# Scattering one coded value per edge and counting over 80 half-target buckets in a graph-transformer kernel

## What is computed

```python
# layer 0, graph part: x is the normalised input, (625, 1024)
out = x @ root + bias
for r in range(8):
    mask = (edge_type == r)
    sums = segment_sum(x[src] * mask, dst, 625)
    cnt = segment_sum(mask, dst, 625)
    out = out + (sums / max(cnt, 1)) @ weight[r]
z = concat([out, x]) @ w_gate + b_gate
h = tanh(out) * z + x * (1 - z)
# beside it: linear attention on x (qkv, 16 heads), then a quantised MLP; layer 1 is of the same kind
```

## Time and profile before

| | us |
|---|---|
| median of 3 runs | 1878.79 |
| lowest, highest | 1878.29, 1881.19 |
| span of the profiled execution | 1878.8 |
| TensorE busy in it | 1794.9 |
| VectorE busy in it | 1023.3 |
| ScalarE busy in it | 478.5 |
| GpSimd busy in it | 701.1 |

### The profile page before, as it was taken

How to read it: one execution, slowest core, us unless ns; L and a number is a source line. 1 busy time by engine, 2 the same in 40 slices (tenths; PEclk the granted TensorE clock), 3 DMA queues, 4 the chain that set the end, 5 groups by cost and what they waited for, 6 DMA issues and landing times.

```text
span 1878.8 us, 28666 instructions
## 1 busy us (share of the span) xinstructions
PE 1794.9 (96%) x9953; PEld 1477.4 (79%) x9953; DVE 1023.3 (54%) x2540; ACT 478.5 (25%) x1055; POOL 701.1 (37%) x609
## 2 busy tenths in 40 slices
PE   6999999999999999999999999954999999999999
PEld 4876689987777778787777887742899888878987
DVE  7888999997254543526354356786632224362311
ACT  3139956662010110101011145243100000111100
POOL 2110000003634435353534444200485552345862
PEclk9999999999999999999999999956999999999999
DMA  4532222224213121231313534110354351113322
GB/s 134 154 109 77 73 86 79 75 67 129 91 38 89 45 72 56 66 86 47 94 33 113 172 84 131 45 46 7 96 164 146 104 156 51 37 55 118 90 73 66
DMA packets 129282, 162.23 MB, mean 86 GB/s; under 512 B 14288, under 2 KB 75368, under 8 KB 128922
## 3 DMA queue, kind: packets, MB, share of 16 engines
q1 hardware_dynamic: 100848, 120.93, 21.5%
q10 hardware_dynamic: 22250, 23.53, 4.0%
q0 software_dynamic: 6080, 16.40, 2.9%
HBM read 135.51 MB, written 25.30 MB: 86 GB/s over the span
## 4 chain that ended last, share of the span: by engine, by line
PE 84%; DVE 6%; ACT 6%; issue 1%; DVEq 1%; DMA 1%; POOL 0%; ACTq 0%; SPq 0%
PE ps L367 22%; PE ps L368 22%; PE ps L369 21%; PE ps L1236 9%; PE ps L892 3%; ACT sc_col L838 2%; ACT sc_row L837 1%; PE ps L1201 1%; DVE w_lo L318 1%; PE ps L881 1%; PE ps L1156 1%; DMA nat<-in_x 1%; ACT w_hi L313 1%; PE ps L1183 1%; PE ps L1211 0%
## 5 line engine op out<-in xcount | busy, mean ns | idle before, releaser
L367 PE MATMUL ps<-w_hi,xt_hi 128*125 128x512 f32 x1320 | 539.0, 408 | 9.1 <-DVE xt_lo L549 3.5
L256 POOL TENSOR_TENSOR w_hi<-w_stage,zero 128x512 fp32r<-128x512 f32 x256 | 276.8, 1081 | 684.4 <-PE ps L369 670.0
L368 PE MATMUL ps<-w_lo,xt_hi 128*125 128x512 f32 x1320 | 523.0, 396 | 0.0
L369 PE MATMUL ps<-w_hi,xt_lo 128*125 128x512 f32 x1320 | 521.5, 395 | 0.0
L259 POOL TENSOR_TENSOR w_lo<-w_stage,w_hi 128x512 fp32r<-128x512 f32 x256 | 346.2, 1352 | 20.1
L367 PEld LDWEIGHTS ps<-w_hi,xt_hi 128*125 128x125 f32 x1320 | 246.6, 187 | 67.1 <-DVE xt_lo L549 4.3
L369 PEld LDWEIGHTS ps<-w_hi,xt_lo 128*125 128x125 f32 x1320 | 246.0, 186 | 63.3
L368 PEld LDWEIGHTS ps<-w_lo,xt_hi 128*125 128x125 f32 x1320 | 246.3, 187 | 53.5
L367 PE MATMUL ps<-xt_hi,w_hi 128*128 128x314 f32 x736 | 250.5, 340 | 1.3 <-DVE ring L2430 0.6
L369 PE MATMUL ps<-xt_hi,w_lo 128*128 128x314 f32 x736 | 225.9, 307 | 0.0
L368 PE MATMUL ps<-xt_lo,w_hi 128*128 128x314 f32 x736 | 225.7, 307 | 0.0
(11 more groups left out here) (392 smaller groups left out, 2390.2 us busy)
## 6 DMA issues: line engine op xcount, KB each, us to landing
w_stage<-in_stream SPq DMA_DIRECT2D x374, 256.0 KB, 2.7
pre<-ring POOLq DMA_DIRECT2D x30, 250.0 KB, 3.8
a_qt<-pre_t SPq DMA_DIRECT2D x18, 312.5 KB, 3.8
a_qt<-pre_t ACTq DMA_DIRECT2D x14, 312.5 KB
pre_t<-ring_t POOLq DMA_DIRECT2D x12, 312.5 KB, 2.8
pre_t<-ring_t ACTq DMA_DIRECT2D x12, 312.5 KB
a_vx<-pre SPq DMA_DIRECT2D x9, 312.5 KB
nat<-pre SPq DMA_DIRECT2D x2, 1250.0 KB
```

Source lines behind the costliest of these rows:

```text
L256: POOL.tensor_tensor(w_hi[:, q, :], w_stage[:, q % NST, :], zero[:].to_broadcast([128, 512]), ALU.add).then_inc(S("hi_done"), 1)
L367: PE.matmul(dst, l_hi, r_hi, start=first, stop=False)
L368: PE.matmul(dst, l_hi, r_lo, start=False, stop=False)
L369: return PE.matmul(dst, l_lo, r_hi, start=False, stop=last)
```

## The change

- Buckets are halved by target: 80 of them, number 2 x (old bucket) + (target is 314 or more). Each is padded to chunks of 128, which again makes 240 chunks, in 120 pairs.
- Positions: the mask has 28 rows in place of 40. Three bucket numbers share a row, with weights 1, 256 and 65536, so that one running sum counts three. A second sum over 80 operations of 166 int16 values (`key_start`) gives each edge the start of its bucket.
- Scatter: target and source are packed in the upper 16 bits of a float32 (`e_code`), so that its bf16 value holds both. VectorE makes the masked table `sc_code` in one operation. ScalarE has no part in it. One matmul of 240 columns in place of two. `slot_keys` unpacks the bits.
- Count: `hot_col` is 314 wide and `hot_row` is made for four chunks at once (512 elements); one matmul of 314 columns for each chunk; one ScalarE copy for each pair; one add of 314 for each chunk, at a start that is read from `g_start` into registers, four at a time (`hist_starts`).
- `adj` is zeroed by VectorE just ahead of the scatter, no longer by ScalarE.
- Groups 0 to 3 are evacuated by ScalarE without a bias (`evacuate_plain`). Their biases are loaded late by SP (`load_bias_h`; the second pair behind a wait for `gsum`) and added by VectorE to `nat` and `z` (`bias_half`).
- GpSimd takes the splitting over at chunk 84 in place of 86.

```diff
     def scatter_dve(c, j):
         DVE.wait_ge(S("sc_pe"), c + 1)
-        if row_on_dve(j):
-            DVE.tensor_scalar(sc_row[j][:], iota16[0:P, 0:128], e_lo[:, bass.ds(c, 1)], e_row1[:, bass.ds(c, 1)],
-                              ALU.is_equal, ALU.mult)
         DVE.tensor_scalar(sc_hi[j][:], iota16[0:P, 0:NCHUNK], e_hi[:, bass.ds(c, 1)], None, ALU.is_equal)
-        DVE.tensor_scalar(sc_lo[j][:], iota16[0:P, 0:128], e_lo[:, bass.ds(c, 1)], None,
-                          ALU.is_equal).then_inc(S("sc_hot"), 1)
+        DVE.tensor_scalar(sc_code[j][:], iota16[0:P, 0:128], e_lo[:, bass.ds(c, 1)],
+                          e_code[:, bass.ds(c, 1)].bitcast(F32), ALU.is_equal, ALU.mult).then_inc(S("sc_hot"), 1)
...
+    def hist_hot(c):
+        if c % 4 == 0:
+            if c >= 8:
+                DVE.wait_ge(S("hi_pe"), c - 4)
+            DVE.tensor_tensor(hot_row[c // 4 % 2][:], iota_by4[:],
+                              slot_row[:, c:c + 4].unsqueeze(1).to_broadcast([128, 128, 4]), ALU.is_equal)
+        if c >= 8:
+            DVE.wait_ge(S("hi_pe"), c - 7)
+        DVE.tensor_scalar(hot_col[c % 8][:], col_key[:], slot_col[:, bass.ds(c, 1)], None,
+                          ALU.is_equal).then_inc(S("hi_dve"), 1)
...
+    def hist_add(c, start):
+        DVE.wait_ge(S("hi_main"), c // 2 + 1)
+        if c:
+            DVE.wait_ge(S("hi_add"), c)
+        o = adj[:, bass.ds(start, SPLIT)]
+        DVE.tensor_tensor(o, o, counts[c // 2 % 4][:, c % 2, :], ALU.add).then_inc(S("hi_add"), 1)
...
+                for c in (2 * (h * per + n), 2 * (h * per + n) + 1):
+                    hist_add(c, starts[c])
+                    if c + LEAD_HOT < NCHUNK:
+                        hist_hot(c + LEAD_HOT)
+                    if c % STARTS == 0 and c + STARTS < NCHUNK:
+                        starts.update(zip(range(c + STARTS, c + 2 * STARTS), hist_starts(c + STARTS)))
+                    if c % 2 == 0 and chunk_at(h, n):
+                        split_dve(chunk_at(h, n))
...
+        for b in range(NKEY):
+            DVE.tensor_scalar(key_start[:, b, :], e_key16[:], float(b), b_off[:, b:b + 1], ALU.is_equal, ALU.mult)
...
+        if c == C_GATE - 3:
+            SP.wait_ge(S("gsum"), 1)
+            load_bias_h(2)
...
     DVE.reciprocal(rgam[:], gam[:])
     DVE.drain().then_inc(S("rgam"), 1)
+    DVE.wait_ge(S("ld_z"), 32)
+    DVE.wait_ge(S("ld_bh"), 64)
+    for g in range(2):
+        bias_half(z, g)
```

More of the change, by code:

```diff
@@ L731, in bucket_counts @@
-        DVE.tensor_tensor_scan(scan[:].rearrange("p b c -> p (b c)"), kh, kh, 0.0, ALU.add, ALU.max)
+        DVE.scalar_tensor_tensor(e_key[:], e_key[:], 2.0, e_half[:], ALU.mult, ALU.add)
+        DVE.drain()
+        k_, row, first = e_key[:], e_row[:, 0:EC], e_first[:, 0:EC]
+        wide, narrow = e_wide[:, 0:EC], e_narrow[:, 0:EC]
+        DVE.tensor_copy(e_key16[:, 0:EC], k_)
+        DVE.tensor_scalar(first, k_, float(NROW), None, ALU.is_ge)
+        DVE.tensor_scalar(e_half[:], k_, float(2 * NROW), None, ALU.is_ge)
@@ L732, in bucket_counts @@
+        DVE.tensor_scalar(e_pos[:], e_col[:], float(SPLIT // 2), float(KEY1 - KEY0 - SPLIT // 2), ALU.is_ge, ALU.mult)
         DVE.drain()
-        DVE.memset(b_beg[:, 0:1], 0.0)
-        DVE.tensor_copy(b_beg[:, 1:NBUCKET], scan[:, 0:NBUCKET - 1, EC - 1])
+        DVE.tensor_tensor(e_col[:], e_col[:], e_pos[:], ALU.add)
+        DVE.scalar_tensor_tensor(row, first, -float(NROW), k_, ALU.mult, ALU.add)
+        DVE.tensor_scalar(wide, first, 2.0 ** 8 - 1.0, 1.0, ALU.mult, ALU.add)
+        DVE.tensor_scalar(narrow, first, 2.0 ** -8 - 1.0, 1.0, ALU.mult, ALU.add)
@@ L735, in bucket_counts @@
         DVE.drain()
-        DVE.tensor_tensor(b_tot[:], scan[:, :, EC - 1], b_beg[:], ALU.subtract)
+        DVE.scalar_tensor_tensor(row, e_half[:], -float(NROW), row, ALU.mult, ALU.add)
+        DVE.scalar_tensor_tensor(wide, e_half[:], 2.0 ** 16 - 2.0 ** 8, wide, ALU.mult, ALU.add)
+        DVE.scalar_tensor_tensor(narrow, e_half[:], 2.0 ** -16 - 2.0 ** -8, narrow, ALU.mult, ALU.add)
+        DVE.drain()
+        DVE.scalar_tensor_tensor(e_low[:], e_col[:], 128.0, e_low[:], ALU.mult, ALU.add)
@@ L910, in beside @@
         for g in range(3):
-            load_bias(g)
-            for c in range((g + 1) * KT, (g + 2) * KT):
+            ahead = (g + 2) * KT - (2 if g == 0 else 1)
+            for c in range((g + 1) * KT, ahead):
                 split_act(c)
-        load_bias(3)
+            evacuate_plain(g)
+            for c in range(ahead, (g + 2) * KT):
+                split_act(c)
         for c in range(C_HAND, C_HAND + 4):
             split_act(c)
-        wait(ALE, mk)
-        mk_zero = sig(ALE.activation(adj[:].bitcast(F32), zero[0:P, :].to_broadcast([P, NBUCKET * NB // 2]), ACT.Copy), "act_step")
+        evacuate_plain(3)
         dense(3)
@@ L952, in beside @@
         DVE.wait_ge(S("split_done"), NST + C_HAND)
[L953 to L956 removed]
+        assert SC0 == G_PLAIN
         for i in range(SC_GROUPS):
@@ L973, in beside, with idle @@
             if i == SC_GROUPS - 1:
[L974 removed]
                 DVE.wait_ge(S("sc_pe"), sc_per + EC + 1)
[L976 to L979 removed]
+                slot_keys()
+                for c in range(LEAD_HOT):
+                    hist_hot(c)
             evacuate(i + SC0)
[L982 to L983 removed]
         HI0 = SC0 + SC_GROUPS
         assert HI0 + HI_GROUPS == G_PRE0
[L986 to L987 removed]
+        per = NPAIR // HI_GROUPS
+        assert per * HI_GROUPS == NPAIR and per * 4 == KT * T * 3
+        def idle(h, s_):
+            return s_ in (1, 2) or s_ > 2 and s_ % 4 == 3 and 3 < s_ < 36 if h == 0 else s_ % (4 if h < HI_GROUPS - 1 else 8) == (
+                3 if h < HI_GROUPS - 1 else 7)
         def hist_of(h, s_):
[L990 to L992 removed]
+            n = sum(not idle(h, i) for i in range(s_))
+            return n if not idle(h, s_) and n < per else None
         def first_step(h, k):
```

392 lines of the change are left out of this document (214 added, 178 removed).

## The result

The changed kernel takes **1865.39 us** (median of four, 1864.44 to 1866.98), the kernel before beside it 1878.68: ratio 0.9925, interval 0.9913 to 0.9937. The forecast was 1866. The median agrees, but three of its terms were off, and their errors cancelled; most of what follows is on them.

A forecast was written before the change was run, and what follows sets the result against it. TensorE, busy in 96% of the span, was taken to bound the kernel, with VectorE pacing the count step. Terms +5.2 - 13.7 + 1 + 0.6 - 7.7 + 2 = -12.6 took 1878.8 to 1866 us; range 1846 to 1902.

The forecast's parts named there:

- Ahead of the scatter: VectorE's work before the scatter: 72.0 us added, 51.1 removed, 8.4 of waits closed; ready at 147.0, +5 us.
- Scatter: In the scatter, VectorE sets the pace at 5.22 us a weight chunk instead of 6.13: -13.7 us.
- clock and transition: Around the scatter: +1 us for TensorE's longer wait and clock, +0.6 for unpacking keys and masks before the count.
- the term of 1 us: At the scatter's start, TensorE's longer wait, about 7 us, costs 1 us more through the granted clock; bounds 0 and 3.
- Count step: In the count step, VectorE's masks, adds, own waits, register loads and splits need 179 us against 186.5: -7.7 us.
- 10.1 us of ends and gaps: In the count step, the part of 186.5 us left to the step's ends and small gaps, kept for the changed kernel.
- Rival (a): Count step: the load costs by the register, 60 loads add 20 to 40 us, giving 1886 to 1906; chance 0.30.
- neighbouring words: Count step: the argument against a load costing by the register, that the four words loaded are neighbours; no size.
- Rival (b): Count step: the wait for the own add is hidden, 0.1 not 0.22; 24 us less, 1842; chance 0.12.
- floor of 155 us: Count step: TensorE's least time, 186.5 us less 31 us for the halved count matmuls.
- Late biases: Late part: adds on z fit VectorE's idle 8.13 us, adds on nat cost nothing, loads delay weight chunks: +2 us.

The follow-up runs named there:

- the two experiments: The changed kernel without the late biases at all, 1856.2 us, and the changed kernel without only the two adds on z, 1861.5 us.

## Why the prediction was right, and where it wasn't

**Ahead of the scatter: the sum held within 3 us.** VectorE was to be ready at 147.0 and was at 150.0. The 80 operations took 14.0 us (7.19 for 41 and 6.84 for 39) against 16. The fill's row has 10.49 us against my 10, but ahead of it VectorE stands still for 2.72 us. These are 2.72, to within 0.01, in all eight traces with the fill at this place, and in the five without it they are gone; so they belong to the fill, which took 13.21 us from the end of the work before to its own end. The trace doesn't say what VectorE does in them. The Trainium skill (VectorE: DVE Perf Modes, Zero memsets can be issued as uint32) gave an estimate of 13.0 us for this fill by one cycle an element; the 13.21 agree, the row's 10.49 (0.84 ns an element) alone doesn't. The other 2 us of the delay I haven't traced to single terms.

**Scatter: right.** 5.17 us a chunk against 5.22, 4.70 for TensorE against 4.7. From the first mask to the first turned matmul the change brought 14.5 us, forecast 12.1 with clock and transition. The mean granted clock of the stretch was 0.98, before 0.97, so nothing shows the term of 1 us for it.

**Count step: right in its mechanism, mis-sized.** 17.1 us came, not 7.7. The distances were to be 0.70, 0.54, 0.54 and 0.78 for four chunks and are 0.62, 0.52, 0.52 and 0.79: 7 us over 60 fours, 5 of them from the load. That distance was summed as 0.05 + 0.45 + 0.2 and is 0.06 + 0.35 + 0.21: the mechanism is the one forecast, and what was too dear is the load, of which I had read 0.45 for one register out of a gap of 0.69. The trace of the kernel before has 0.30 for it, and for the one in that gap 0.32. The splits cost 16 against 15. And 10.1 us of ends and gaps were carried over unchanged, where about 5 remain: 168.0 us less 60 x 2.45 and 16. The step before was also 1.4 us shorter than I took it (to 427.5, not 428.8), which works the other way.

**Rival (a)** was refuted in size: by medians 60 loads cost some 4 to 6 us, and near 8 with the stray long ones. The reason against it (neighbouring words) isn't shown to be one; what hides most of a load is the add in front, whose end is awaited in any case. Its mechanism shows at eight registers. The Trainium skill (Runtime: NRT & Kernel Launch, Instruction fetch mechanics) gave 0.2 us a register; here, for words in SBUF, 0.06 was measured between four and eight, and a load of two took longer than one of four, so the trace doesn't agree.

**Rival (b)** didn't happen (0.52, not 0.45), but its price was near: 19 us where the wait was taken away, 24 named. Its floor of 155 us was wrong, since it was worked out from a step in which TensorE was taken to be full.

**Late biases: the step that failed.** "Those on z stand where VectorE idles 8.13 us and need 5.5" was the wrong test. The idle time was VectorE's, but GpSimd worked in it, on the chunks that TensorE waited for; beside it the adds are not free: 3.2 us, where I had put nothing. And the loads, taken at 2 us, cost 4.1 in the two experiments. Together 6.4 to 10.5 us, outside the bounds of 0 and 5 that I had set.

**The errors cancelled**: 9.4 us more gain from the count step; against it 4.4 in the late part, 0.9 in the search, 0.6 up to the scatter's end, and 2.8 between spans and medians. 1866 was right by its mechanisms in the first half of the program and by luck in the rest.

## What to carry to other kernels

An idle stretch of an engine is cover only if no other engine does work in it that shares something with the new operations and is awaited; look at who works there, not only at who rests. Where an instruction waits for the one just before it of its kind on its own engine, what the sequencer has to do in between, a load of registers above all, comes out on the time as far as it outlasts that instruction; two targets by turns hide both. And work that is moved to an idle engine goes to a place in its queue, not to the engine: the same fill was worth nothing at one place and 9.7 us at another, some 3 us later.

## What was not expected of the hardware

- Three subtractions of 128 x 512 on GpSimd took 3.8 us alone and 8.7 where VectorE had float32 additions of 125 x 2560 beside two of them and a clip of 128 x 2048 beside the third. The second addition took 3.90 in place of 2.83, the clip 2.28 in place of 1.27.
- A register load of one word took 0.30 us, of two 0.53, of four 0.34, of eight 0.60.
- A fill of 125 x 12521 float32 on VectorE has a row of 10.49 us, and 2.72 us of standing still ahead of it that come and go with it.
- A late stretch of the same code lost between 6.4 and 10.5 us, in step with the moment at which its weight chunks could be split.
